# Four reorderings around the routing of a mixture of experts: weight splits, a gate's activation, two matmuls and two result adds

## The chip, the cores and the metric

The kernel runs on one core of one Trainium2 chip. The metric is the device time of one launch in microseconds (us), lower is better. The program is written engine by engine: TensorE (PE) multiplies, VectorE (DVE), ScalarE (ACT) and GpSimd (POOL) do the rest, SyncE (SP) issues transfers. Each engine runs its own instruction list in order and waits on semaphores that the others raise.

## The reference, cut to what matters

The reference is one layer: a cross attention, a state-space block beside an MLP, and then a mixture of experts on 1024 tokens of 512 features. Only the last part is touched. With `h` the normalised tokens:

```python
logits = h @ gate_weight.T                       # 8 experts
scores = softmax(logits)
topk_w, topk_i = group_limited_topk(scores)      # best 2 of 4 groups, then best 2 experts
g = einsum('th,nfh->ntf', h, gate_w); u = einsum('th,nfh->ntf', h, up_w)
e = einsum('ntf,nhf->nth', silu(g) * u, down_w)  # F = 352
routed = einsum('nth,tn->th', e, wmat)
shared = silu(h @ sh_gate_w.T) * (h @ sh_up_w.T) @ sh_down_w.T   # FS = 704
x = x + routed + shared
```

## The kernel before, in words

`phase_experts` handles the mixture as 39 steps of 128 tokens each. Steps 0 to 7 apply the first half of the shared expert's 704 features to the eight token tiles (weight set 0), steps 8 to 30 apply the routed experts to 23 tiles of tokens sorted by expert (sets 1 to 8), and steps 31 to 38 apply the other half of the shared expert (set 9). A step is `gate(j)`, `turn_hidden`, `up(j)`, `down(j)` on PE: twelve matmuls of 352 columns, twelve more, three transposes of the hidden rows, nine matmuls of 512 columns. Every product is made of three passes (high by high, high by low, low by high; lines 43 to 45), so every operand is split into a high and a low part. PE's list is software pipelined: at index `j` it runs `gate(j+1)`, `turn_hidden(j)`, `up(j+1)`, `down(j)`.

For each step ACT makes the activation of the gate (`gated`, line 2259) and the high part of the turned hidden rows (`hidden_hi`, line 2265); DVE makes the product of gate and up (`product`, line 2321), the low part of the hidden rows (`hidden_lo`, line 2325), and adds the step's result to `x` (`keep_results`, line 2354). `down(j)` waits for `hidden_lo(j)` (`hlo_ok`), and because the result has two buffers, for `keep_results(j-2)` (`y_ok`).

The routing is spread between the first steps. PE makes the logits during step 0. DVE's routing comes in pieces, `route.vector(v, m)`: m = 0 softmax, m = 1 groups, m = 2 the comparison of experts (lines 1910 to 1912), the choice (1917 to 1919) and running sums (1944), m = 3 the place of each token (1951 to 1965), m = 6 the tables of tiles, m = 5 the weights. Between m = 2 and m = 3 PE does two small matmuls, `tensor_places` (lines 1867 and 1870). At the end of m = 3 the slots are known (`slot_ok`), and POOL issues 16 indirect transfers of 256 KB each (line 2124) that write the normalised rows to their slots in memory. SP waits for all 16, then loads the first four sorted tiles (line 2081). PE turns the first of them (`turn_rows(0)`, line 2210) at index 6, between `up(7)` and `down(6)`; nothing behind it on PE can start before.

Weights arrive in one raw buffer of three pieces (gate, up, down). ACT makes the high part and DVE the low part of sets 0 and 1 (`split`, lines 2282 to 2285 and 2359 to 2363), POOL those of later sets, beginning after its scatters. SP issues the load of a piece of set k+1 when that of set k has been split (`piece_free`, lines 2070 to 2074). Set 1's three pieces are split by ACT at indices 1, 2 and 3 and by DVE at indices 2, 3 and 4, so the gate and up pieces of set 2 are loaded then.

Of the kernel before, what the change touches and what calls it, by code (L numbers as in the profile page):

```python
# [1802 lines left out]
NW, RING = 3, 3  # L1803
# [13 lines left out]
def route_programs(n, far, d, g):  # L1817
# [77 lines left out]
    def vector(v, m):  # L1895
# [39 lines left out]
                                 grank[:].rearrange("p t (g o) -> p t g o", o=1).to_broadcast([P, TT, NG, NE // NG]), ALU.mult))  # L1935
        if m == 2:
            compare(masked, NE)
            fewer_than_two(chosen, NE).then_inc(chosen_ok, 1)
            v.wait_ge(chosen_ok, 1)
            v.wait_ge(pads, 3)  # L1940
            for i in range(3):
                a, far_back = counted[i], 2 ** i
                out = counted[i + 1][:, 2 * far_back:2 * far_back + TT, :] if i < 2 else upto[:]
                v.tensor_tensor(out, a[:, far_back:far_back + TT, :], a[:, 0:TT, :], ALU.add).then_inc(summed, 1)
                v.wait_ge(summed, i + 1)
            link(v.tensor_tensor(masked[:], chosen[:], masked[:], ALU.mult))
        if m == 3:
            v.wait_ge(pos_ready, 1)
            places, held_by = psum[:, LB, 0:TT * NE].rearrange("p (t e) -> p t e", e=NE), psum[:, LB, TT * NE:(TT + 1) * NE]
            full = compared[:, 0, 0:NE * EXT].rearrange("p (e j) -> p e j", j=EXT)  # L1950
            link(v.tensor_tensor(full, held_by.rearrange("p (e o) -> p e o", o=1).to_broadcast([P, NE, EXT]), steps_of[:], ALU.is_gt))
            link(v.tensor_reduce(tiles[:], full, AX_X, ALU.add))
            over = compared[:, 0, 0:NE * NE].rearrange("p (e f) -> p e f", f=NE)
            link(v.tensor_tensor(over, before[:], tiles[:].rearrange("p (o f) -> p o f", o=1).to_broadcast([P, NE, NE]), ALU.mult))
            link(v.tensor_reduce(start[:], over, AX_X, ALU.add))

            link(v.scalar_tensor_tensor(out=pos[:], in0=start[:].rearrange("p (o e) -> p o e", o=1).to_broadcast([P, TT, NE]),
                                        scalar=float(SLOTS), in1=places, op0=ALU.mult, op1=ALU.add))

            link(v.scalar_tensor_tensor(out=held[:], in0=pos[:], scalar=-float(NT * SLOTS), in1=chosen[:], op0=ALU.add, op1=ALU.mult))  # L1960
            link(v.tensor_reduce(slot_f[:, 0, :], held[:], AX_X, ALU.min))
            link(v.tensor_scalar(slot_f[:, 0, :], slot_f[:, 0, :], float(NT * SLOTS), None, ALU.add))
            link(v.tensor_tensor(held[:], pos[:], chosen[:], ALU.mult))
            link(v.tensor_reduce(slot_f[:, 1, :], held[:], AX_X, ALU.max))
            v.tensor_copy(slot[:], slot_f[:]).then_inc(slot_ok, 1)
# [38 lines left out]
def phase_experts(nc, d, g, far, scan):  # L2004
# [8 lines left out]
    with ExitStack() as ctx:  # L2013
# [134 lines left out]
        @block.tensor  # L2148
        def _(pe):
            place = {}  # L2150

            def tokens(j):
                if routed(j):
                    return [a[:, (j - TT) % 2, :, :] for a in (tT_hi, tT_lo)]
                t = j % TT if j < TT else j - TT - NT
                return [a[:, :, t * P:(t + 1) * P] for a in (xT_hi, xT_lo)]

            def find_weights(j):
                if j == 0:
                    pe.wait_ge(first_ok, 2)  # L2160
                if j == TT:
                    pe.wait_ge(route.tables_ok, 1)
                if routed(j):
                    r = j - TT
                    need = pe.value_load(route.order[0:1, 0, r:r + 1], min_val=NW, max_val=NW * NE)
                    at = pe.value_load(route.order[0:1, 1, r:r + 1], min_val=0, max_val=RING - 1)
                    place[j] = bass.ds(at, 1)
                    pe.wait_ge(w_ok, need)
                else:
                    place[j] = slice(0, 1)  # L2170
                    if j == TT + NT:
                        pe.wait_ge(w_ok, NW * LAST)

            def features(j, i, bank):
                hi, lo = tokens(j)
                for dc in range(DC):
                    m = passes(pe, psum[:, bank + j % 2, 0:FE], hi[:, dc, :], lo[:, dc, :],
                               *(a[:, place[j], i, dc, :].rearrange("p o f -> p (o f)") for a in (w1_hi, w1_lo)),
                               dc == 0, dc == DC - 1)
                return m  # L2180

            def gate(j):
                find_weights(j)
                if routed(j):
                    pe.wait_ge(xlo_ok, j - TT + 1)

                wait(pe, s_ok, j - 1)
                features(j, 0, GB).then_inc(g_ready, 1)

            def up(j):  # L2190

                wait(pe, h_ok, j - 1)
                features(j, 1, UB).then_inc(u_ready, 1)

            def turn_hidden(j):
                pe.wait_ge(h_ok, j + 1)

                wait(pe, hlo_ok, j)
                f0 = 0
                for c, wd in enumerate(WD):  # L2200
                    m = pe.transpose(psum[0:wd, HB, c * P:(c + 1) * P], h[:, f0:f0 + wd], g["ident"][:])  # L2201
                    f0 += wd
                m.then_inc(ht_ready, 1)

            def turn_rows(r):
                pe.wait_ge(x_in[r % XR], 16 * (r // XR + 1))

                wait(pe, xlo_ok, r)
                for c in range(DC):
                    m = pe.transpose(psum[:, XB, c * P:(c + 1) * P], x_rows(r)[:, c * P:(c + 1) * P], g["ident"][:])  # L2210
                m.then_inc(xt_ready, 1)

            def down(j):
                if j == 0:
                    pe.wait_ge(first_ok, NW)
                pe.wait_ge(hlo_ok, j + 1)

                wait(pe, y_ok, j - 1)
                for c, wd in enumerate(WD):
                    m = passes(pe, psum[:, DB + j % 2, :], hT_hi[0:wd, c, :], hT_lo[0:wd, c, :],  # L2220
                               *(a[0:wd, place[j], c, :].rearrange("p o k -> p (o k)") for a in (w2_hi, w2_lo)),
                               c == 0, c == NC - 1)
                m.then_inc(dn_ready, 1)
            scan.tensor(pe)

            pe.wait_ge(scan.o_ok, TT - 1)
            norm.transpose_tile(pe, TT - 2)
            route.tensor_first(pe, 0)

            pe.wait_ge(scan.ms_ok, TT)  # L2230
            gate(0)
            norm.transpose_tile(pe, TT - 1)
            up(0)
            pe.wait_ge(norm.lo_done, TT)
            route.tensor_first(pe, 1)
            for j in range(STEPS):
                if j + 1 < STEPS:
                    gate(j + 1)
                if j == 0:

                    pe.wait_ge(scan.o_ok, TT)
                turn_hidden(j)
                if j == 0:
                    route.tensor_logits(pe)
                if j + 1 < STEPS:
                    up(j + 1)
                if j == 1:
                    route.tensor_places(pe)
                if routed(j + 2):
                    turn_rows(j + 2 - TT)  # L2250
                down(j)

        @block.scalar
        def _(act):
            def gated(j):
                act.wait_ge(g_ready, j + 1)

                wait(act, h_ok, j)
                act.activation(s[:], psum[:, GB + j % 2, 0:FE], ACT.Silu).then_inc(s_ok, 1)  # L2259
# [30 lines left out]
            norm.high_part(act, TT - 2)  # L2290
            act.wait_ge(scan.o_ready, TT)
            split(0, 2)
            gated(0)
            norm.high_part(act, TT - 1)
            route.scalar_first(act)
            for j in range(STEPS):
                if j + 1 < STEPS:
# [5 lines left out]
                    store_results(j - 1 - TT)  # L2303
                if j:
                    hidden_hi(j)
                if j - 1 in range(NW):
                    split(1, j - 1)
                if routed(j + 2):
                    r = j + 2 - TT
                    rows_hi(r)  # L2310
# [4 lines left out]
        def _(v):  # L2315
# [64 lines left out]
            split(0, 2)  # L2380
            norm.low_part(v, TT - 1)
            product(0)
            later = {0: 2, 1: 3, 2: 6, 3: 5}
            for j in range(STEPS):
                hidden_lo(j)
                if j == 0:
                    route.vector(v, 0)
                    route.vector(v, 1)
                if j + 1 < STEPS:
                    product(j + 1)  # L2390
                if j in later:
                    route.vector(v, later[j])
                if j - 2 in range(NW):
                    split(1, j - 2)
                if routed(j + 2):
                    rows_lo(j + 2 - TT)
                t = j - TT - NT
                if t >= 1:
                    v.wait_ge(y_ok, j)
                    add_back(t - 1)  # L2400
                    if t == TT - 1:
                        add_back(t)
                keep_results(j)


def second_columns(nc, ctx, tag):
# [160 lines left out]
```

## Time and profile before

| | |
|---|---|
| median of 3 runs | 1013.42 us (1009.63 to 1014.2) |
| profiled execution | 1011.37 us, span 1009.5 us |
| PE busy | 956.6 us, 95% |
| DVE, ACT, POOL busy | 530.1, 413.0, 453.4 us |
| experts begin, end | about 735 us to the end of the span |

The span is what the trace covers of the profiled execution; what lies around it is 1.87 us. A row of a timeline gives the start of an instruction, its duration, engine, line, operation, output and inputs, and in brackets the idle time of the engine before it with what ended it. Successive instructions of one engine can overlap by about 0.1 us, and PE's matmuls overlap by about half.

### The profile page before, as it was taken

The numbers are of one execution on the slowest core, as the hardware profiler recorded it, in microseconds if no ns is written. First come the engines' busy times: TensorE is split into PE (matmuls) and PEld (weight loads), VectorE is DVE, ScalarE is ACT, GpSimd is POOL, SyncE is SP. The second block draws the span as 40 slices with busy tenths as digits, with TensorE's granted clock in tenths as the row PEclk, the third lists the DMA queues.
The fourth block names the chain that finished last, engine by engine and source line by source line (L and its number), as shares of the span: only waits on it lengthen the run. The fifth ranks groups of instructions, "written<-read, shape, count | busy, mean of one in ns | idle before, by whom it ended". The sixth has DMA issues, their size and how long they took to land. (4 is left out here: it accounts for less than half of the span.)

```text
span 1009.5 us, 15936 instructions
## 1 busy us (share of the span) xinstructions
PE 956.6 (95%) x5497; PEld 807.7 (80%) x5497; DVE 530.1 (53%) x975; ACT 413.0 (41%) x956; POOL 453.4 (45%) x489
## 2 busy tenths in 40 slices
PE   6999977999899989999999999989999999999987
PEld 5777756888778868888888988767779899999977
DVE  4443358777788735454444223338866333333335
ACT  1444458777878724343222233543332122222111
POOL 1798866555667510000000303137607978990041
PEclk9999999999999999999999999999999999999989
DMA  7499813111111105223310025220016656751142
GB/s 248 159 269 266 239 55 95 43 43 38 38 32 41 46 1 188 84 83 101 125 45 21 14 59 156 88 100 2 23 65 210 224 194 204 231 184 50 52 145 96
DMA packets 79003, 109.92 MB, mean 109 GB/s; under 512 B 14224, under 2 KB 46992, under 8 KB 78928
## 3 DMA queue, kind: packets, MB, share of 16 engines
q1 hardware_dynamic: 66288, 82.18, 26.7%
q10 hardware_dynamic: 10080, 18.35, 5.2%
q0 software_dynamic: 2560, 8.39, 2.5%
q8 instruction: 46, 0.75, 0.3%
q14 instruction: 29, 0.24, 0.1%
HBM read 83.13 MB, written 25.77 MB: 108 GB/s over the span
## 5 line engine op out<-in xcount | busy, mean ns | idle before, releaser
L43 PE MATMUL psum<-second_xT_hi,second_w_hi 128*128 128x512 f32 x272 | 106.8, 393 | 4.9 <-PEq L74 2.9
L45 PE MATMUL psum<-second_xT_hi,second_w_lo 128*128 128x512 f32 x272 | 106.0, 390 | 0.0
L44 PE MATMUL psum<-second_xT_lo,second_w_hi 128*128 128x512 f32 x272 | 106.0, 390 | 0.0
L1239 POOL TENSOR_TENSOR all_x<-all_x,mlp_raw 128x512 f32<-128x512 f32 x8 | 10.0, 1288 | 173.1 <-DVE all_x L1741 173.1
L2259 ACT ACTIVATE moe_s<-psum 128x352 f32<-128x352 f32 x39 | 18.1, 465 | 156.1 <-PE psum L45 136.8
L2325 DVE TENSOR_TENSOR moe_hT_lo<-psum,moe_hT_hi 128x384 fp32r<-128x384 f32 x39 | 21.7, 558 | 83.0 <-ACT moe_hT_hi L2265 83.0
L43 PEld LDWEIGHTS psum<-second_xT_hi,second_w_hi 128*128 128x128 f32 x272 | 51.0, 188 | 17.4 <-issue 3.5
L1696 ACT ACTIVATE mlp_s<-psum,mlp_side 128x512 f32<-128x512 f32 x32 | 21.8, 682 | 100.2 <-PE psum L45 100.2
L43 PE MATMUL psum<-moe_w_hi,moe_tT_hi 128*128 x184 | 61.3, 333 | 0.0
L1741 DVE TENSOR_TENSOR all_x<-all_x,psum 128x512 f32<-128x512 f32 x64 | 43.8, 686 | 31.6 <-PE psum L45 31.2
L45 PEld LDWEIGHTS psum<-second_xT_hi,second_w_lo 128*128 128x128 f32 x272 | 51.1, 188 | 10.8
L44 PEld LDWEIGHTS psum<-second_xT_lo,second_w_hi 128*128 128x128 f32 x272 | 51.1, 188 | 10.5
L45 PE MATMUL psum<-moe_w_hi,moe_tT_lo 128*128 x184 | 59.2, 322 | 0.0
L44 PE MATMUL psum<-moe_w_lo,moe_tT_hi 128*128 x184 | 59.0, 320 | 0.0
L43 PE MATMUL psum<-moe_w_hi,moe_hT_hi 128*128 (+3 forms) x117 | 49.2, 421 | 5.7 <-DVE moe_hT_lo L2325 5.7
L43 PE MATMUL psum<-q_G_hi,att_cT_hi 128*128 128x512 f32 x128 | 52.9, 413 | 0.9 <-DVE all_x L1037 0.9
L2106 POOL TENSOR_TENSOR moe_w_lo<-far_raw,moe_w_hi 128x1408 fp32r<-128x1408 f32 x16 | 51.9, 3244 | 0.0
L44 PE MATMUL psum<-q_G_lo,att_cT_hi 128*128 128x512 f32 x128 | 50.5, 395 | 0.0
L45 PE MATMUL psum<-mix_wo_hi,mix_wo_lo 128*128 128x512 f32 x128 | 49.9, 390 | 0.0
L43 PE MATMUL psum<-mix_wo_hi 128*128 128x512 f32 x128 | 49.9, 390 | 0.0
L44 PE MATMUL psum<-mix_wo_lo,mix_wo_hi 128*128 128x512 f32 x128 | 49.8, 389 | 0.0
L1735 DVE TENSOR_TENSOR mix_wo_lo<-mlp_s,mix_wo_hi 128x512 fp32r<-128x512 f32 x32 | 22.1, 691 | 51.5 <-ACT mix_wo_hi L1702 51.5
(344 smaller groups left out, 2868.3 us busy)
## 6 DMA issues: line engine op xcount, KB each, us to landing
kv_all<-all_x ACTq DMA_DIRECT2D x28, 256.0 KB, 4.9
far_raw<-in_eg SPq DMA_DIRECT2D x10, 704.0 KB
far_raw<-in_eu SPq DMA_DIRECT2D x10, 704.0 KB
slot_rows<-mix_W SPq DMA_DIRECT2D x23, 256.0 KB, 5.9
slot_out<-far_rows ACTq DMA_DIRECT2D x23, 256.0 KB, 2.3
far_raw<-in_ed SPq DMA_DIRECT2D x10, 512.0 KB
far_rows<-slot_rows ACTq DMA_DIRECT2D x19, 256.0 KB, 3.3
second_raw<-in_w_feat SPq DMA_DIRECT2D x18, 256.0 KB, 3.5
```

The source lines that it names most:

```text
L43: e.matmul(out, hi_l, hi_r, start=first, stop=False)
L44: e.matmul(out, hi_l, lo_r, start=False, stop=False)
L45: return e.matmul(out, lo_l, hi_r, start=False, stop=last)
L1239: pool.tensor_tensor(g["x"][:, t, :], g["x"][:, t, :], b2, ALU.add).then_inc(x_plus, 1)
L1696: act.activation(s1[:, m % 2, :], psum[:, UP + m % 4, :], ACT.Gelu_apprx_tanh, bias=side[:, p, c:c + 1]).then_inc(act_ok, 1)
L1735: v.tensor_tensor(h_lo[:, c, half * HALF:(half + 1) * HALF], s1[:, m % 2, :], h_hi[:, c, half * HALF:(half + 1) * HALF].bitcast(F32), ALU. ...
L1741: v.tensor_tensor(x[:, t, :], x[:, t, :], psum[:, DN + t % 4, :], ALU.add).then_inc(dn_ok, 1)
L2106: pool.tensor_tensor(w1_lo[:, u, i, :, :], raw1[:, i, :, :], w1_hi[:, u, i, :, :].bitcast(F32), ALU.subtract).then_inc(w_ok, 1)
L2259: act.activation(s[:], psum[:, GB + j % 2, 0:FE], ACT.Silu).then_inc(s_ok, 1)
L2325: v.tensor_tensor(hT_lo[:], psum[:, HB, 0:NC * P].rearrange("p (c k) -> p c k", k=P), hT_hi[:].bitcast(F32), ALU.subtract).then_inc(hlo_ok, 1)
```

## The change

Four lists are reordered; nothing is computed that was not computed before.

```diff
@@ route_programs.vector
         if m == 2:
             compare(masked, NE)
+        if m == 3:
             fewer_than_two(chosen, NE).then_inc(chosen_ok, 1)
...
-        if m == 3:
+        if m == 4:
             v.wait_ge(pos_ready, 1)
@@ tensor
-                if j == 1:
-                    route.tensor_places(pe)
                 if routed(j + 2):
                     turn_rows(j + 2 - TT)
                 down(j)
+                if j == 1:
+                    route.tensor_places(pe)
@@ scalar
             split(0, 2)
+            split(1, 0)
             gated(0)
             norm.high_part(act, TT - 1)
+            split(1, 1)
             route.scalar_first(act)
...
-                if j - 1 in range(NW):
-                    split(1, j - 1)
+                if j == NW:
+                    split(1, NW - 1)
@@ vector
             product(0)
-            later = {0: 2, 1: 3, 2: 6, 3: 5}
+            split(1, 0)
+            split(1, 1)
+            later = {0: 2, 1: 4, 2: 6, 3: 5}
             for j in range(STEPS):
                 hidden_lo(j)
                 if j == 0:
                     route.vector(v, 0)
                     route.vector(v, 1)
+                if j == 1:
+                    route.vector(v, 3)
                 if j + 1 < STEPS:
                     product(j + 1)
                 if j in later:
                     route.vector(v, later[j])
-                if j - 2 in range(NW):
-                    split(1, j - 2)
+                if j == NW + 1:
+                    split(1, NW - 1)
+                if j == 1:
+                    keep_results(0)
...
-                keep_results(j)
+                if j:
+                    keep_results(j)
```

So on DVE the order after the comparison becomes: `hidden_lo(1)`, choice and sums (now m = 3), `product(2)`, places (now m = 4), `keep_results(0)`, `keep_results(1)`. On PE `down(1)` stands ahead of the two matmuls of `tensor_places`. The gate and up pieces of set 1 are split before index 0 on both engines; its down piece stays at index 3 on ACT and 4 on DVE.

## Rows read from the trace of the kernel before

**Rows 1.** Chain that ended last, 735 to 800 us: start, duration, what.

```profile
782.36 3.92 DMA slot_rows<-far_rows,moe_slot
786.29 2.78 DMA far_rows<-slot_rows
```

**Rows 2.** Timeline of PE around the places, and the first turned rows.

```profile
749.20 0.32 PE L43 MATMUL psum<-moe_w_hi,moe_xT_hi 128*128 128x352 f32 x1
...
753.23 0.32 PE L45 MATMUL psum<-moe_w_hi,moe_xT_lo 128*128 128x352 f32 x1
...
755.00 0.43 PE L1870 MATMUL psum<-moe_upto,far_earlier 128*128 128x64 f32 x2 [0.34 <-DVE moe_upto L1944]
756.45 0.50 PE L43 MATMUL psum<-moe_w_hi,moe_hT_hi 128*128 128x512 f32 x1 [1.01 <-DVE moe_hT_lo L2325]
...
758.64 0.32 PE L43 MATMUL psum<-moe_w_hi,moe_xT_hi 128*128 128x352 f32 x1
...
789.12 0.66 PE L2210 MATMUL psum<-all_ident,far_rows 128*128 128x128 f32 x4 [0.98 <-DMA far_rows<-slot_rows]
```

**Rows 3.** Timeline of DVE through the routing.

```profile
745.17 0.56 DVE L2325 TENSOR_TENSOR moe_hT_lo<-psum,moe_hT_hi 128x384 fp32r<-128x384 f32 x1 [4.98 <-ACT moe_hT_hi L2265]
...
752.52 0.69 DVE L1917 TENSOR_TENSOR moe_compared<-moe_compared 128x512 f32<-128x512 f32 x1
...
755.24 0.69 DVE L2354 TENSOR_TENSOR all_x<-all_x,psum 128x512 f32<-128x512 f32 x1
755.84 0.55 DVE L2325 TENSOR_TENSOR moe_hT_lo<-psum,moe_hT_hi 128x384 fp32r<-128x384 f32 x1
756.31 0.51 DVE L2321 TENSOR_TENSOR moe_h<-moe_s,psum 128x352 f32<-128x352 f32 x1
756.74 0.22 DVE L1951 TENSOR_TENSOR moe_compared<-psum,far_steps_of 128x64 f32<-128x64 f32 x1
...
759.24 0.17 DVE L1965 CAST moe_slot<-moe_slot_f 128x16 uint32<-128x16 f32 x1
```

**Rows 4.** Timeline of ACT: the first gate, and the hidden rows of step 1.

```profile
737.23 0.47 ACT L2259 ACTIVATE moe_s<-psum 128x352 f32<-128x352 f32 x1 [2.64 <-PE psum L45]
...
752.17 0.49 ACT L2265 ACTIVATE moe_hT_hi<-psum 128x384 fp32r<-128x384 f32 x1
```

**Rows 5.** Timeline of POOL: four of the 16 scatters, the first and the longest.

```profile
759.72 1.22 POOL L2124 DMA_INDIRECT slot_rows<-far_rows,moe_slot  x1 [23.81 <-DVE moe_slot L1965]
...
766.49 2.35 POOL L2124 DMA_INDIRECT slot_rows<-far_rows,moe_slot  x1 [0.30 <-issue]
...
771.68 2.11 POOL L2124 DMA_INDIRECT slot_rows<-far_rows,moe_slot  x1 [0.30 <-issue]
...
776.65 1.58 POOL L2124 DMA_INDIRECT slot_rows<-far_rows,moe_slot  x1 [0.30 <-issue]
```

**Rows 6.** Timeline of DVE: low parts of set 1, beside the scatters.

```profile
766.38 1.62 DVE L2359 TENSOR_TENSOR moe_w_lo<-far_raw,moe_w_hi 128x1408 fp32r<-128x1408 f32 x1
...
771.33 1.62 DVE L2359 TENSOR_TENSOR moe_w_lo<-far_raw,moe_w_hi 128x1408 fp32r<-128x1408 f32 x1
...
776.17 1.22 DVE L2361 TENSOR_TENSOR moe_w_lo<-far_raw,moe_w_hi 128x1024 fp32r<-128x1024 f32 x1
777.31 0.68 DVE L2362 TENSOR_TENSOR moe_w_lo<-far_raw,moe_w_hi 96x512 fp32r<-96x512 f32 x1
```

**Rows 7.** View of the tile `slot_rows`: durations in ns (minimum, median, maximum), and landings.

```profile
L2124 POOL DMA_INDIRECT slot_rows<-far_rows,moe_slot x16: 965/971/2345, 759.7 to 782.4; - x16
...
DMA to landing us min/median/max: 2.6/5.4/7.0
```

**Rows 8.** DMA busy tenths from 728 to 748 us, a digit per 0.5 us.

```profile
DMA  0005569961008399810000589991000000000000
```

**Rows 9.** Timelines of ACT and PE near 970 us.

```profile
969.05 0.46 ACT L2259 ACTIVATE moe_s<-psum 128x352 f32<-128x352 f32 x1 [8.53 <-remote]
...
971.61 0.80 PE L43 MATMUL psum<-moe_w_hi,moe_hT_hi 128*128 128x512 f32 x1 [3.47 <-DVE moe_hT_lo L2325]
...
975.62 0.49 PE L43 MATMUL psum<-moe_w_hi,moe_xT_hi 128*128 128x352 f32 x1
```

**Rows 10.** Window: us, busy us of PE, PEld, DVE, ACT, POOL; granted clock; DMA share; GB/s.

```profile
971.00:972.00 1.00, 0.39 (x1) 0.39 (x2) 1.00 (x3) 0.00 (x0) 0.00 (x0) 0.50 0.05 21
```

## The prediction

> **What bounds the kernel now.** I began with the chain that ended last, which says where the end is set. Through the experts it lies on PE, except between about 744 and 789 us: there it runs through the routing on DVE, the 16 scatters on POOL, the landing of the last scatter (3.92 us) and the load of the first sorted tile (2.78 us) [rows 1]. Then I read PE's timeline for what this costs PE. It stands idle in two places. The first is around the places. The last matmul of `up(2)` starts at 753.23 and frees the array 0.16 later, at 753.39; `down(1)` begins only at 756.45 and `gate(3)` at 758.64 [rows 2]. `tensor_places` waits for DVE's choice and sums, and `down(1)`, queued behind it, then waits for `hidden_lo(1)`. The second is `turn_rows(0)`: 0.98 us until 789.12, for the sorted rows [rows 2]. So two paths arrive at 789 almost together, PE 1 us ahead of the scatters. Speeding one alone is worth 0 (PE) or at most 1.0 us (scatters); the change touches both.
>
> **PE: `down(1)` ahead of the places.** It needs `hidden_lo(1)`. ACT ends the high part at 752.17 + 0.49 = 752.66 [rows 4]. In the new order DVE has done only the comparison by then, which ended where L1917 begins, 752.52 [rows 3]. So `hidden_lo(1)` runs from about 752.69 to 753.24 and PE sees it 0.06 later (before, 756.39 and 756.45): 753.30, ahead of 753.39. `down(1)` starts without a wait and takes 758.64 - 756.45 = 2.19 [rows 2], or 2.1 without its slow first matmul: until 755.5.
>
> DVE goes on 0.47 after it started `hidden_lo(1)` (755.84 to 756.31 [rows 3]), at 753.16. Choice, sums and the masked weights take 755.24 - 752.52 = 2.72, so `product(2)` starts at 755.88, and the last sum, one instruction of 0.26 before that, is in at 755.60. The second matmul of the places starts at about 755.7, bound by PE's own queue as much as by DVE, and takes 0.43 [rows 2]. `gate(3)` starts at about 756.1, where it was 758.64: 2.5 us earlier.
>
> **What is late next.** `gate(3)`, `turn_hidden(2)` and `up(3)` take what their forerunners took, 753.39 - 749.20 = 4.19 [rows 2], so `down(2)` could begin at 760.3. It waits for `hidden_lo(2)`, which on DVE now stands behind the places and two result adds. `product(2)` 755.88, places from 755.88 + 0.43 = 756.31 (PE's answer is in at 756.15), `keep_results(0)` after 759.24 - 756.74 + 0.08 = 2.58, at 758.89, `keep_results(1)` 0.60 later, `hidden_lo(2)` at 760.09, done at 760.64 [rows 3]. PE starts `down(2)` at 760.70, plus 0.1 for a first matmul after a wait. Before it started at 758.64 + 4.19 = 762.83. The gain on PE is 2.1 us, not 2.5. `keep_results(0)` itself is needed by `down(2)`, at 759.6: in time. From index 2 on DVE has two splits of 1.62 fewer, so no later `hidden_lo` is late. PE comes to `turn_rows(0)` at 789.12 - 0.98 - 2.1 = 786.05.
>
> **The splits ahead of the routing.** ACT stands idle 2.64 us before its first gate at 737.23 [rows 4]. The load of set 1's gate piece was issued when DVE had split that of set 0, and its transfer is the first burst, over by 733.0; the second, the up piece, is over by 737.0 [rows 8]. A gate piece takes ACT 1.4 us: from 734.6 to 736.0, before 737.23. The up piece, after the last norm tile at 738.3, ends before 740, and ACT's next work comes at 742.4. DVE stands idle 4.98 us before 745.17, from 740.2 [rows 3], and the two low parts take 2 x 1.62 = 3.24 [rows 6]: done by 743.5, with 1.7 us in hand. Both cost nothing here. Without that cover each 1.62 would fall on the routing chain. The issue of set 2's gate and up pieces on SP moves with them, from 768 and 773 to about 742 and 743.5; from 742 to 748 the DMA engines were idle [rows 8], and nothing in SP's list stands between.
>
> **The scatters.** A scatter takes 0.97 us at the median [rows 7] and 0.30 to the next. Three are long: 2.35, 2.11 and 1.58 [rows 5], 1.38 + 1.14 + 0.61 = 3.13 us over the rest. Each began while DVE was making a low part of set 1, and each ended 0.84 us after that instruction: 766.38 + 1.62 = 768.00 and 768.84; 772.95 and 773.79; 777.39 and 778.23 [rows 5, 6]. Three times the same 0.84 is no chance. The change takes the first two splits away, so 2.52 go. The third stays at index 4, 2.1 us earlier, at 774.05 to 775.27. On the new grid a scatter begins at 774.9 to 775.0 and would be held 0.15 to 0.3 instead of 0.61. I count nothing for it, and bound it between 0.5 gained and 0.5 lost.
>
> The Trainium skill ("SBUF — State Buffer", the section on the two physically separate sides) says that a VectorE instruction with two SBUF inputs and a GpSimd one share a port pair by an exclusive lock, held for the whole instruction. By its words whoever starts first wins and the other fully blocks; here the second instruction of the third split (777.31) did not hold POOL again, since the scatter was under way, and its own 0.68 was not stretched. If a scatter fell between the two parts and were held by the second one, the third split would cost up to 0.9 us instead of 0.3. That bound would put the first row at 786.9 at the latest.
>
> The slots are known 0.43 us earlier (L1951 at 756.31, not 756.74 [rows 3]). The last scatter is issued at 782.36 - 0.43 - 2.52 = 779.4. Its landing took 3.92 then, while the loads of set 2 shared the engines; the least of the 16 was 2.6 [rows 1, 7]. Now only the down piece's load falls in the train. Between 2.6 and 3.92 I take 3.1, nearer to the least, since two of three loads are gone: 782.5. The first sorted tile is in 2.78 later, at 785.3, within 784.5 and 786.6 over both bounds and the third split. PE comes at 786.05. So PE is likely not held, or for a few tenths, and both idle spots go.
>
> **Sum.** PE resumes at 786.05 instead of 789.12: 3.1 us, 2.5 at worst by these bounds. Behind it everything that PE could wait for is POOL's splitting, which starts 2.9 us earlier as well, and no wait for weights was seen. So 1009.5 becomes 1006.4 in span and 1011.37 becomes 1008.3 in the profiled execution's own time. That execution lies 2.05 us below the median of the runs, so for the median 1013.42 - 3.1 = 1010.3.
>
> **Rivals.**
> *The wait only moves.* PE gains 2.1, but the rows come as late as before but for 0.43, because the long scatters have another cause (a descriptor buffer that fills, say) and would recur. Against it stand the three equal 0.84. It gives 0.4 us: 1013.0.
>
> *The hole at 970 goes.* ACT's gate activation came at 969.05 after 8.53 us of waiting for something the trace calls remote, PE waited 3.47 [rows 9], and afterwards its granted clock stood at 0.50, that is 1.2 GHz [rows 10]: the nine matmuls of `down` took 975.62 - 971.61 = 4.01 us [rows 9] instead of 2.19, and the next gate began slow too (0.49 instead of 0.32 a matmul), some 2.5 us. In all 6 us. It lies beside POOL's gathers and is not touched, but it is no data wait that I can name, and may come and go by execution: 3.1 + 6 gives 1004.3. The Trainium skill ("Runtime: NRT & Kernel Launch", instruction fetch mechanics) says engines fetch instructions by a DMA queue of their own and mostly hide it; this hole is what an unhidden fetch would look like, and no row proves it.
>
> *Slower: such a hole opens in another place.* The loads of set 2 now run at 742 to 747, a stretch in which no data moved and in which the chain runs through ACT and DVE. If one engine's remote wait of the kind of [rows 9] falls there, or the one near 970 grows to twice its size, 6 us are lost against 3.1 won: 1016.3. It decides from a hold of 3.1 us on the chain. Against it: between 728 and 742 loads ran beside the same engines [rows 8] without one.
>
> **How the numbers follow.** The forecast (2.5 to 3.4 us gained) has 0.62, the moved wait and values between 0.3 and 2.5 us 0.20, the vanished hole 0.10, the new hole 0.08. The likeliest case is 1010.3. The runs of before spread over 4.6 us, more than the gain, so the median of a few can lie 2 us to either side. The range that leaves out 2 in 10 is 1005.5 to 1013.5. Half a per cent is 5.1 us, about what tells from no change. The forecast lies inside it; with the spread of the runs 0.12 of it goes beyond, and with the vanished hole faster gets 0.22. Slower gets 0.06 of the new hole and the spread, and 0.72 is left for no change.
>
> **What would show it.** Right: on PE, `down(1)` about 0.1 us behind the last matmul of `up(2)`, `gate(3)` near 756.1, an idle spot of about 0.4 us ahead of `down(2)` released by L2325, and none or under 0.5 us ahead of L2210 at about 786. On POOL, a first scatter at 759.3, no scatter of 2.1 to 2.4 us, at most one over 1.3, and a train of 20 instead of 22.6 us to the start of the last. On SP, the loads of set 2 at about 742 and 743.5. Wrong: long scatters without a split beside them; a wait of over 1 us ahead of L2210; ACT's first gate after 737.3 or `hidden_lo(0)` after 745.3, which would mean that the early splits are on the path.

## The result, and the profile after

The changed kernel takes 1022.18 us (median of 8 runs, 1019.21 to 1024.27), the kernel before 1013.81 us beside it (8 runs, 1009.63 to 1027.34). The ratio is 1.0084, 95% interval 1.0064 to 1.0105: slower by 8.4 us, where 3.1 us less was forecast. The profiled execution took 1023.44 us with a span of 1021.6 us; its mean granted clock was 0.984, where that of before was 0.994.

I compared the start of the same PE instruction in both traces, after minus before:

| point | before | after | difference |
|---|---|---|---|
| first 370 us | | | -0.9 to +0.9 |
| 700 to 755 us | | | +4.5 |
| `gate(3)` | 758.64 | 760.49 | +1.85 |
| `down(2)` | 762.83 | 765.32 | +2.49 |
| `down(4)` | 775.48 | 788.25 | +12.8 |
| `turn_rows(0)` | 789.12 | 802.32 | +13.2 |
| end | 1009.5 | 1021.6 | +12.1 |

First the 4.5 us that lie far ahead of the change. The difference is 0.9 us at 370 us; another 1.5 and 2.8 us come in two stretches in which the granted clock of the changed kernel stood at 0.50 (1.2 GHz), which the windows of both kernels show (0.7 is made good between them). Each line is a stretch, its length, the busy time (and count) of PE, weight load, DVE, ACT and POOL, then clock, DMA share and GB/s. The first block is after, the second before, over the same work:

```profile
378.43:381.84 3.41, 3.11 (x7) 2.48 (x8) 1.40 (x5) 0.00 (x0) 1.94 (x3) 0.50 0.47 125
675.39:682.21 6.82, 6.11 (x15) 4.94 (x16) 4.97 (x5) 2.46 (x3) 6.09 (x6) 0.50 0.83 307
```

```profile
377.00:381.00 4.00, 3.26 (x17) 2.73 (x17) 1.40 (x5) 0.00 (x0) 2.09 (x3) 1.00 0.45 126
672.00:679.00 7.00, 5.97 (x85) 4.74 (x86) 5.29 (x4) 4.08 (x4) 4.74 (x5) 1.00 0.95 331
```

The instructions there are the same in both kernels, and such slow stretches come in some executions of before too (e10 below, which is the kernel before, was at 0.50 from 671.1 to 677.9); I leave them out of the account of the change. Within the change's own part, 4.5 us (4.55 just ahead of `gate(3)`) has to be taken off every time of after.

There the forecast's steps came as written. PE's timeline after (start, duration, engine, line, operation, output and inputs, in brackets the idle time before and its end):

```profile
760.28 0.40 PE L1870 MATMUL psum<-moe_upto,far_earlier 128*128 128x64 f32 x2
760.49 0.41 PE L43 MATMUL psum<-moe_w_hi,moe_xT_hi 128*128 128x352 f32 x1
...
765.32 0.50 PE L43 MATMUL psum<-moe_w_hi,moe_hT_hi 128*128 128x512 f32 x1 [0.43 <-DVE moe_hT_lo L2328]
...
771.50 0.32 PE L45 MATMUL psum<-moe_w_hi,moe_xT_lo 128*128 128x352 f32 x1
...
773.52 0.39 PE L45 MATMUL psum<-moe_w_hi,moe_hT_lo 96*128 96x512 f32 x1
...
775.51 0.33 PE L45 MATMUL psum<-moe_w_hi,moe_xT_lo 128*128 128x352 f32 x1
775.67 0.49 PE L2202 MATMUL psum<-all_ident,moe_h 128*128 128x128 f32 x3
...
777.78 0.32 PE L45 MATMUL psum<-moe_w_hi,moe_xT_lo 128*128 128x352 f32 x1
788.25 0.80 PE L43 MATMUL psum<-moe_w_hi,moe_hT_hi 128*128 128x512 f32 x1 [10.16 <-DVE moe_hT_lo L2328]
```

Both waits around the places [rows 2] are gone: `gate(3)` gained 4.55 - 1.85 = 2.7 us, `down(2)` waits 0.43 us, and 4.55 - 2.49 = 2.1 us of gain stay. The last line is the loss: PE stands idle for 10.16 us ahead of `down(4)`, where before it had no wait. `up(5)` ended at 778.1, and PE's next instruction had to wait.

POOL's groups by line give the count, least, median and longest duration in ns, and the first and last start; and SP's queue the issues of set 2's loads:

```profile
L2125 POOL DMA_INDIRECT slot_rows<-far_rows,moe_slot x16: 968/972/1225, 763.9 to 783.3; - x16
```

```profile
746.29 0.34 SPq L2071 DMA_DIRECT2D far_raw<-in_eg  x1
747.82 0.33 SPq L2071 DMA_DIRECT2D far_raw<-in_eu  x1
```

The long scatters of [rows 5] are gone. The 16 now form one train without a break, a start each 1.28 us, 19.4 us to the start of the last instead of 22.64.

What held PE? DVE's `hidden_lo(4)` was released by ACT, which waited for PE's transposes and `gate(5)`. Timelines of ACT and DVE through the hole:

```profile
786.76 0.46 ACT L2260 ACTIVATE moe_s<-psum 128x352 f32<-128x352 f32 x1 [14.84 <-remote]
```

```profile
774.02 0.52 DVE L2324 TENSOR_TENSOR moe_h<-moe_s,psum 128x352 f32<-128x352 f32 x1 [2.96 <-remote]
...
778.31 0.69 DVE L2357 TENSOR_TENSOR all_x<-all_x,psum 128x512 f32<-128x512 f32 x1 [2.35 <-remote]
```

Compare them with when PE ended that work, in the fence of PE above. `up(4)` ended at 771.8 and DVE's product of it came at 774.02; `down(3)` ended at 773.9 and its result add came at 778.31; `gate(5)` ended at 775.8 and ACT's activation came at 786.76, 11 us later and 2.5 us after the last scatter's instruction (783.32 + 0.97). So the data was there and the word of it was late. "Remote" is how the trace writes a release that it can't put down to an instruction: [rows 9] shows the same, 8.53 us, near 970. That hole too lies in such a train, 10 gathers (indirect transfers that read the sorted results back) at 1.25 us, without a break but not quite without a stall: the sixth took 1.35 us instead of 0.95. After the change it is still there, the sixth gather first, then ACT:

```profile
975.66 1.38 POOL L2146 DMA_INDIRECT far_rows<-slot_out,moe_slot  x1 [0.30 <-issue]
977.34 0.95 POOL L2146 DMA_INDIRECT far_rows<-slot_out,moe_slot  x1 [0.30 <-issue]
```

```profile
982.16 0.47 ACT L2260 ACTIVATE moe_s<-psum 128x352 f32<-128x352 f32 x1 [8.61 <-remote]
```

The windows show that apart from POOL no engine was busy for more than 1.05 of 10 us in the new hole, and what followed. Of PE only the end of one matmul lies in the first; over the second the clock was at 0.50, and a 128x512 matmul took 0.63 us where 0.39 is usual:

```profile
778.00:788.00 10.00, 0.09 (x1) 0.00 (x0) 1.05 (x2) 0.84 (x2) 4.85 (x5) 0.66 0.42 159
```

```profile
781.20:791.44 10.24, 3.19 (x8) 2.52 (x9) 2.72 (x4) 0.84 (x2) 3.50 (x4) 0.50 0.26 97
```

The hole cost 10.3 us (2.49 to 12.8), the slow matmuls behind it 1.5; the wait for the first sorted rows (0.98 in [rows 2]) was gone, which gave 1.0 back. The sum over the change's part: -2.1 + 10.3 + 1.5 - 1.0 = +8.7 us; a shorter slow stretch behind the late hole takes it to 7.6 at the end (12.1 - 4.5). The medians differ by 8.4.

### The profile page after: what moved, and what is told of

It reads as the page before. It is cut to its first block and busy times, and to the rows that moved or that the text cites. A ratio compares the mean times of both kernels' runs of the same rounds, so it can differ in the third digit from the quotient of the medians.

```text
span 1021.6 us, 15937 instructions
## 1 busy us (share of the span) xinstructions
PE 961.2 (94%) x5497; PEld 811.1 (79%) x5497; DVE 531.6 (52%) x975; ACT 413.3 (40%) x956; POOL 451.0 (44%) x489
```

## The experiments

Four chips are on record for the experiments: Q (e1 to e4), R (e5 to e8, e17, e18), S (e9 to e12) and T (e13 to e16). Which one the pair above ran on is not; it is called P, and may be a fifth or one of these. "Before" is always the kernel before on the same chip. The theory after the first pair: POOL's unbroken train of indirect transfers holds back PE's signals (the semaphore counts by which ACT and DVE learn that a matmul is done); before, three scatters stalled behind DVE's splits [rows 5, 6] and so broke it. Rivals: the order of the lists does it, or set 2's loads at 742 us.

**Halves of the change.** e1 keeps the new order with the splits where they were; e2 does only the early splits:

```diff
@@ e1, against the changed kernel (ACT; DVE alike)
-            split(1, 0)
-            split(1, 1)
-                if j == NW:
-                    split(1, NW - 1)
+                if j - 1 in range(NW):
+                    split(1, j - 1)
```

> Only the reordering of DVE's and PE's lists around the places; set 1 is split where it was before, so its three low parts still interrupt the scatters. Theory T1 (PE's signals are held when POOL issues more than about six scatters without a break): the scatters keep their breaks of 1.38, 1.14 and 0.61 us, no hole near 778, PE 2.1 us earlier up to the wait for the sorted rows, of which 0.4 remains: 1013 against 1013.8 of before, ratio 0.9995. Theory T2 (the new order itself opens the hole, whatever the scatters do): a hole of about 10 us ahead of down(4), 1022. Theory T3 (early loads of set 2 open it): as T1.

> Only the two early splits; the order around the places is that of before. T1: the scatters come in one train of 1.28 us each, a hole of some 10 us on PE with 1.2 GHz behind it opens as in the changed kernel, 12 us less 1 us of the rows' wait: 1022 to 1025. T2: no hole, scatters 2.5 us shorter, 1 us gained: 1012.8. T3: as T1.

e1: 1009.55 against 1010.64 us, ratio 0.9991 [0.996, 1.0022]. e2: 1020.64, ratio 1.0125 [1.006, 1.0191]. The splits alone bring the whole loss. In e1 three scatters stalled again, and PE has no wait between `down(2)` and the rows; in e2 PE waited 8.54 us. POOL of e1 (two of its three long ones), then ACT of e2:

```profile
764.95 1.50 POOL L2125 DMA_INDIRECT slot_rows<-far_rows,moe_slot  x1 [0.30 <-issue]
...
770.59 1.49 POOL L2125 DMA_INDIRECT slot_rows<-far_rows,moe_slot  x1 [0.30 <-issue]
```

```profile
780.37 0.46 ACT L2259 ACTIVATE moe_s<-psum 128x352 f32<-128x352 f32 x1 [13.21 <-remote]
```

This leaves two differences, the loads that move with the splits and the unbroken train.

**Breaks in the trains.** e3 is the changed kernel, in which POOL does two of its own splits of set 2 (1.37 us each) after the 5th and 10th scatter instead of after the 16th. e4 is the kernel before with a copy of 1.37 us, whose result nobody reads, after the 3rd, 6th and 9th gather of each late train.

```diff
@@ e3, after a scatter on POOL
+                    if TOP * t + i + 1 in (5, 10):
+                        split(2, -1 - (5, 10).index(TOP * t + i + 1))
@@ e4, after a gather on POOL
+                    if TOP * t + i + 1 in (3, 6, 9):
+                        pool.tensor_copy(w1_hi[:, 1 + i, (t & 1), :, :], raw1[:, 0, :, :])
```

> The changed kernel, with POOL's high parts of set 2's gate and up pieces (1.37 us each) moved between its scatters, after the fifth and after the tenth. Loads of set 2 stay early. T1: no hole near 778; the last scatter is issued 2.7 us later than in the changed kernel, PE waits about 2 us for the rows: gain of 0.5 to 1.5 us over before, 1012.5. T2 and T3: the hole stays, 1022 or more.

> The kernel before, with a copy of 128x1408 elements on POOL (1.37 us, its result is never read) after gathers 3, 6 and 9 at the end. T1: the hole of 3.5 us near 970 and the 1.2 GHz behind it go: about 6 us, 1008. If the hole there comes from something else than an unbroken run of indirect transfers: it stays, 1013.8, or 1015 if the gathers' delay shows.

e3: 1010.49 us, ratio 0.9992 [0.9957, 1.0027], on the chip on which e2 lost 10 us; no hole near 778, with set 2's loads as early as in e2 (issued at 740.03 and 741.57; e2 739.57 and 741.10). So the early loads alone don't open the hole. DVE's third split made one more stall there, a scatter of 1.40 us. The price of the breaks is a wait of 1.09 us for the rows. e4: 1008.22 us, ratio 0.9972 [0.9943, 1.0001]; the hole near 970 is gone, and across that stretch its PE gained 6.3 us on the profile of before (5.3 us behind it at 965, 0.9 ahead at 980; another chip). The medians differ by 2.4 us only, and the interval reaches 1.0001, so the forecast gain of 6 us is not shown for the whole kernel. POOL of e4 in the gathers, and PE of e1, which on the same chip kept the hole:

```profile
964.20 0.95 POOL L2145 DMA_INDIRECT far_rows<-slot_out,moe_slot  x1 [0.30 <-issue]
965.14 1.38 POOL L2148 CAST moe_w_hi<-far_raw 128x1408 fp32r<-128x1408 f32 x1
966.70 0.97 POOL L2145 DMA_INDIRECT far_rows<-slot_out,moe_slot  x1 [0.17 <-issue]
```

```profile
970.15 0.80 PE L43 MATMUL psum<-moe_w_hi,moe_hT_hi 128*128 128x512 f32 x1 [3.54 <-DVE moe_hT_lo L2326]
```

**How much of a break.** Four versions of the changed kernel: e5 one break of 1.37 us after scatter 8; e6 a POOL instruction of 0.20 us after scatters 5 and 10; e7 no break, but each scatter waits until the third before it has landed; e8 the breaks of e3 and e4 together.

```diff
@@ e6
+                    if TOP * t + i + 1 in (5, 10):
+                        pool.tensor_tensor(rest[:, t:t + 1], norm.power[:, 0:1], norm.power[:, 0:1], ALU.add)
@@ e7
+                    m = TOP * t + i
+                    wait(pool, scattered[m % 3], 16 * (m // 3))
```

> The changed kernel with one break of 1.37 us (POOL's high part of set 2's gate piece) after the eighth scatter, so two runs of eight. In the changed kernel PE's signals were first late at the seventh or eighth scatter, and at the seventh of the gathers. If the length of an unbroken run decides (T1): PE is held only for the last one or two of each eight, under 2 us in all, no 10 us hole. If the hold comes from the whole amount of scatters in a stretch whatever the breaks: the hole stays near 10 us.

> The changed kernel with one tiny POOL instruction (one element a partition, 0.2 us) after scatters five and ten. If any other POOL instruction between scatters ends the run (something is drained when the kind of work changes): no hole. If a break must last (the pace decides): the hole of about 10 us stays.

> The changed kernel with three semaphores for the scatters; scatter m waits until scatter m-3 has landed (2.6 to 3 us after its issue, so at 1.28 us a scatter the wait costs little). If the hold comes from too many scatters in flight: no hole. If it comes from the pace of issue alone (T1 proper): the pace stays 1.28 us and the hole stays, about 1022.

> The changed kernel with the two breaks among the scatters (useful work) and three among the gathers. T1: what the two single kernels gave adds up, 2.9 us and 5.5 us in the experts' stage: ratio to before 0.992, 1002.5 at a before of 1010.6. If the gathers' breaks only paid because the rest was as before: 0.997.

| | median, us | before | ratio | holes |
|---|---|---|---|---|
| e5 | 1004.20 | 1007.60 | 0.9963 [0.9938, 0.9987] | none |
| e6 | 1004.88 | 1007.60 | 0.9968 [0.994, 0.9997] | none |
| e7 | 1006.07 | 1007.60 | 0.999 [0.9965, 1.0014] | none |
| e8 | 1005.69 | 1007.60 | 0.9976 [0.9956, 0.9996] | none |

All looked like cures, which was too good: no kernel had even the hole near 970, though the gathers of e5 to e7 have no break, and before itself was 3 to 6 us faster than on P and Q. So chip R may not make such holes at all, and the four prove nothing without the changed kernel beside them.

**The same on chip S, with controls.** e9 is the changed kernel, e10 the kernel before, e11 is e7's kernel, e12 is e6's.

> The changed kernel itself, on another chip than its first profile. In the last four runs, all on one chip, the late hole near 970 was gone too, though nothing near it was changed: the holes may belong to some chips alone. If the hole is the kernel's (T1): ratio to before 1.008, PE held some 10 us near 778. If it is the chip's: on a chip without it, the changed kernel runs 2 to 3 us under before, ratio 0.997.

> The kernel before itself, profiled on the same chip as e9. It tells whether this chip shows the late hole near 970 (ACT's gate activation 3 us late beside the gathers). Time: ratio 1.0 to before. With a hole here and none near 970 in e5 to e8, the chips differ; without one here, this chip is of their kind.

> The kernel of e7 (scatter m waits for the landing of m-3) on the same chip as e9. If e9 shows the hole and this doesn't, the number in flight or the wait itself opens it, not the pace. If both show it, the pace does, and e7's good result was its chip's. If neither shows it, this chip says nothing on it.

> The kernel of e6 (a 0.2 us POOL instruction after scatters five and ten) on the same chip as e9. Where e9 shows the hole: none here if any other POOL instruction ends the run of scatters, the same 10 us hole if a break has to last.

e9: 1023.15 us, ratio 1.0081 [1.0032, 1.013]: the first result again. e11: 1022.8, ratio 1.0117 [1.0045, 1.0189], and e12: 1021.31, ratio 1.0102 [1.0016, 1.0188], of two runs each. PE of e9, then of e11, then of e12:

```profile
785.89 0.79 PE L43 MATMUL psum<-moe_w_hi,moe_hT_hi 128*128 128x512 f32 x1 [9.73 <-DVE moe_hT_lo L2328]
```

```profile
785.02 0.79 PE L43 MATMUL psum<-moe_w_hi,moe_hT_hi 128*128 128x512 f32 x1 [9.74 <-DVE moe_hT_lo L2331]
```

```profile
785.71 0.79 PE L43 MATMUL psum<-moe_w_hi,moe_hT_hi 128*128 128x512 f32 x1 [9.75 <-DVE moe_hT_lo L2331]
```

Three holes of one size: neither the limit of three in flight nor two instructions of 0.20 us change it. The limit was a weak test, though: POOL waited for a landing once in e11, 0.47 us ahead of the thirteenth scatter, so the train was nearly the same, and it shows that the hole needs no more than about three scatters in flight. The two "cures" of chip R were the chip.

e10 was meant as a plain control: 1011.5 us, ratio 0.9978 [0.9929, 1.0027]. But its profiled execution (span 1017.6, clock 0.984) had the hole, in the kernel before, here in pieces: PE was 1.7 us behind the first profile at 770.6, 8.9 at `down(4)` and 11.9 at `down(5)`. Its POOL has no scatter over 1.23 us, and PE's signals were late; POOL, then ACT of e10:

```profile
766.61 0.97 POOL L2124 DMA_INDIRECT slot_rows<-far_rows,moe_slot  x1 [0.30 <-issue]
767.88 0.96 POOL L2124 DMA_INDIRECT slot_rows<-far_rows,moe_slot  x1 [0.30 <-issue]
769.15 1.23 POOL L2124 DMA_INDIRECT slot_rows<-far_rows,moe_slot  x1 [0.30 <-issue]
```

```profile
771.38 0.46 ACT L2259 ACTIVATE moe_s<-psum 128x352 f32<-128x352 f32 x1 [6.82 <-remote]
782.93 0.46 ACT L2259 ACTIVATE moe_s<-psum 128x352 f32<-128x352 f32 x1 [9.25 <-remote]
```

PE and DVE of e10 say why the stall failed to come:

```profile
756.70 0.79 PE L43 MATMUL psum<-moe_w_hi,moe_hT_hi 128*128 128x512 f32 x1 [1.01 <-DVE moe_hT_lo L2325]
```

```profile
767.88 1.66 DVE L2359 TENSOR_TENSOR moe_w_lo<-far_raw,moe_w_hi 128x1408 fp32r<-128x1408 f32 x1
```

PE's `down(1)` ran slow (0.79 where 0.50 is usual [rows 2]), so DVE's first split began at 767.88 instead of 766.38 [rows 6]. It ended at 769.54 and found a scatter issued 0.39 before that, which it held for 0.26 us, not for the 1.38 of [rows 5]; the second split began at 779.89, when the last scatter had been issued. A stall that depends on where a DVE instruction falls on a grid of 1.28 us is a matter of luck, and without it the kernel before has the hole as well. It also settles the two rivals better than e3 does: this hole opened in the old order, with set 2's loads late (769.57 and 781.55).

It was no single case. Of the executions of before, 2 of 8 on P, 1 of 25 on Q and 6 of 22 on S took over 1017 us; of 85 on R and T none took over 1011.5. Only e10's was profiled, so that the others had the hole too is a guess.

**Chip T, with the changed kernel as control.** e13 is the changed kernel, e14 is e3's, e15 e5's and e16 e8's.

> The changed kernel as control of its chip: with the hole of about 10 us the three kernels beside it can be judged, at a ratio near 1.008; without it (a chip of the kind of e5 to e8) the ratio is 0.997.

> The kernel of e3 (breaks of 1.37 us after scatters 5 and 10). If breaks of such a length keep PE's signals free (T1): no hole where e13 has one, ratio 0.997 to 1.000. If e3's good result was its chip's: the hole as in e13, 1.008.

> The kernel of e5 (one break of 1.37 us after scatter 8). T1 with a limit of about six or seven: signals late by 1 to 3 us around scatters 7, 8, 15 and 16, between e13 and e14, ratio 1.000 to 1.004. If only breaks as such count: as e14. If breaks do nothing: as e13.

> The kernel of e8 (breaks among scatters and gathers). T1: neither hole, ratio 0.992 where e13 has both. If breaks do nothing: as e13, or 1 us more.

| | median, us | before | ratio |
|---|---|---|---|
| e13 changed | 1004.09 | 1007.57 | 0.9962 [0.9935, 0.9988] |
| e14 | 1006.11 | 1007.57 | 0.9986 [0.9965, 1.0006] |
| e15 | 1005.86 | 1007.57 | 0.9986 [0.9965, 1.0008] |
| e16 | 1004.3 | 1007.57 | 0.9974 [0.9952, 0.9996] |

Here the changed kernel is faster than before, by 3.5 us, with the very same train. POOL's group with the landings of the 16 scatters, then PE at `down(2)` and at the first sorted rows, then ACT near 979, all of e13:

```profile
L2125 POOL DMA_INDIRECT slot_rows<-far_rows,moe_slot x16: 968/972/1224, 757.0 to 776.6; - x16
...
DMA to landing us min/median/max: 2.7/2.8/4.8
```

```profile
758.41 0.50 PE L43 MATMUL psum<-moe_w_hi,moe_hT_hi 128*128 128x512 f32 x1 [0.40 <-DVE moe_hT_lo L2328]
...
783.53 0.60 PE L2211 MATMUL psum<-all_ident,far_rows 128*128 128x128 f32 x4
```

```profile
979.04 0.47 ACT L2260 ACTIVATE moe_s<-psum 128x352 f32<-128x352 f32 x1 [5.44 <-PE psum L45]
```

No hole, no wait for the rows, and near 979 ACT is released by PE after its usual 5.4 us. Against the profile of before, PE is 2.35 us ahead just before the change's part and 5.59 at `turn_rows(0)`: 3.2 us gained there. The breaks, which are good for nothing here, cost e14 a wait of 1.5 us for the rows and e15 one of 0.2.

**A last pair.** e17 is the changed kernel and e18 e3's kernel, to have both on a chip with holes.

> The changed kernel as control once more: e13 to e16 fell on a chip without the hold (the changed kernel had no hole and ran at 0.996 of before). On a chip with it: hole of about 10 us, ratio 1.008. Without: 0.996.

> The kernel of e3 beside the control e17. If e17 shows the hole: none here if 1.37 us breaks after five and ten scatters prevent it (T1), ratio 0.997 to 1.000; the same hole if e3's good result was its chip's. If e17 shows none: 0.998, and this pair says nothing on the hole.

They fell on chip R: e17 1004.87 us against 1007.32, ratio 0.9968 [0.994, 0.9996], no hole; e18 1005.48, ratio 0.9993 [0.9969, 1.0018]. So the changed kernel has no hole on R either, and e5 to e8 were no cures; it does not give the pair that I wanted.

**What the traces lost.** A further look at the traces shows a second difference between the chips. Each of the 16 scatters raises the semaphore `scattered` (e7 and e11 have three) by 16 in steps of 1, and where none is lost each step has a record in the trace, 256 in all.

| profiles | records of 256 |
|---|---|
| ten on R and T | 255 or 256 |
| four on P and Q with breaks or stalls (before, e1, e3, e4) | 160, 98, 111, 161 |
| six on P, Q and S with the hole (after, e2, e9, e10, e11, e12) | 55 to 67 |

That is why the landing line of e13 has no counterpart in the profile after. On P, Q and S records get lost during the trains, most where the hole is. So the theory has a rival that no run tests: the crowded path may be that of the trace's own records. Every execution timed here carries a span and a granted clock, which a trace gives; whether a launch without recording has the hole is not known.

## Why the prediction was wrong

*What held.* On PE `gate(3)` stands 0.2 us behind the second matmul of the places, the wait ahead of `down(2)` is 0.43 us (0.4 forecast), and the gain there 2.1 us (2.1). The scatters: no scatter over 1.23 us (at most one over 1.3), 19.4 us of train (20); but the third split, which was to fall beside them, came only at 788, behind the hole. The loads of set 2 at 746.29 and 747.82, less 4.5 us 741.8 and 743.3 (742 and 743.5). The wait of 0.98 us for the rows gone. The splits on ACT and DVE delayed nothing: `hidden_lo(0)` began at 749.71, that is 745.2 (745.17 [rows 3]). On chips T and R the sum came out as well: 3.2 us in e13's profile and ratios of 0.9962 and 0.9968, that is 3.8 and 3.2 us of 1007.57 and 1007.32, where 3.1 was forecast.

*Slips that changed nothing.* The prediction took 2.6 us for "the least of the 16" landings. The line in [rows 7] covers every transfer of the tile `slot_rows`; none of the 16 scatters has a landing in that trace. In e13 they took 2.7 to 4.8 us and the last was seen by SP after 3.9 (776.63 to 780.51), where the sum has 3.1. With 3.9 the rows come at 786.1, as PE does, so that slip costs under 0.1 us. And "2.5 at worst" leaves out the sum's own later bound of 786.9, by which it is 2.2.

*The Trainium skill's rule* ("SBUF — State Buffer", the section on the two physically separate sides) stood beside the three long scatters. Here the trace agrees: without a low part of set 1 on DVE beside them none was long, and in e1, with these back, the long ones were (1.50, 1.49, 1.73 us). That such a stall is nothing but cost was my own reading; the page doesn't say it.

*What failed.* The step "The scatters" counted the 2.52 us of stalls as gain and asked nothing of what a train without them does to the others. The stalls were also the only breaks in it. The row that said so was in my hands: the remote wait near 970 [rows 9] stands inside ten gathers at 1.25 us without a break (one stall of 0.40), and the prediction says "it lies beside POOL's gathers and is not touched", takes it for a thing that comes and goes, and even puts up a rival in which it goes. What the runs show in its place: with the stalls gone, PE stood idle for 10.16 us ahead of `down(4)`. The rival that came true is "such a hole opens in another place". It has the kind right (a remote wait of the kind of [rows 9], 1.2 GHz behind it), but not the place or the cause: it ties it to set 2's loads at 742 to 747, and it came at 778 in the scatters, as long as the train went on. Priced 6 us, it cost 10.3 + 1.5 us; given 0.08, it stands in both profiles of the changed kernel on chips P and S.

*How sure the cause is.* Shown: the early splits bring the loss (e1, e2 on one chip). Their loads are not it: e3 has them early without a hole, e10 late with one. The new order isn't needed (e2, e10). More than about three scatters in flight aren't needed (e11), and pauses of 0.20 us don't help (e12). A gather train with breaks of 1.37 us loses its hole (e4, e1). On a chip with holes an unbroken train had one in all six profiles (the first pair's, e2, e9, e10, e11, e12), and a train with breaks or stalls of 0.5 us and more had none in four (before on P, e1, e3, e4). That is a pattern over ten profiles; that the missing breaks are the cause is argued from it. Not shown: that breaks alone cure the changed kernel, since no chip with holes ran e3's or e5's kernel beside the changed one, and e3 and e2 differ in the order too. Nor what the scatters and PE's signals share, whether recording has a part in it, nor why chips P, Q and S make such holes and R and T don't: the lost records are those by which the path could be read. Which chip a run would get was unknown ahead, so a forecast from the profile of before alone, a chip with a hole near 970, had to reckon with it.

*Another reading that doesn't hold.* The prediction cited the Trainium skill ("Runtime: NRT & Kernel Launch", instruction fetch mechanics) for the hole near 970 as an unhidden fetch. From 960 to 972 us the trace of before has no instruction packet at all. In the new hole there is one, of 1.1 us at 776.95; e9 has it too, 0.94 us at 775.0. But e17, the same kernel on a chip without holes, has it at the same point of PE's work, 0.94 us at 776.0. The packets' lines for 3 us around it, after and then e17:

```profile
q8 instruction: 1, 0.02, 2.3%
```

```profile
q8 instruction: 1, 0.02, 1.9%
```

The transfer of the fetch takes as long in e17, without a hole, as in e9, with one, so this fetch doesn't explain a wait from 775.8 to 786.8.

*A better version?* On chips without holes the changed kernel itself is the best that ran (0.9962, 0.9968); on T the breaks cost it 0.2 to 2.0 us in the medians; on R e5 was 0.7 us lower and e18 0.6 higher, within the spread. On a chip with holes the best was e4 (0.9972), whose interval reaches 1.0001. The changed kernel with both breaks (e8, e16) never ran on such a chip, so I can't name one that beats both everywhere.

## What to carry to other kernels

A stall that you remove may have been what kept a queue from running unbroken: before counting it as gain, look for another place of the trace in which the same instructions already run without a break, and read what the other engines wait for there. Suspect that a wait called remote that ends with another engine's train of DMA issues belongs to that train. When a cure works, run the disease beside it on the same chip: e6 looked like 0.3% gained (e7 like 0.1%), and both were 1% lost on another. And count the records of a trace before reading a wait in it: where records are missing, the recording may have a part in the wait.

## What the runs showed of the hardware

- On chips P, Q and S, 16 indirect scatters issued by POOL every 1.28 us without a break went with late completions of TensorE as seen by ACT and DVE, later as the train ran: after the change 2.2 us at 774, 4.4 at 778.3, 11 at 786.8. On R and T the same train delayed nothing, and the whole kernel before was faster there by 3 to 6.5 us (1007.3 to 1007.6 against 1010.6 to 1013.8).
- Of the 256 steps by which the scatters raise their semaphore, traces on R and T hold 255 or 256, traces on P, Q and S 55 to 67 with the hole and 98 to 161 without.
- Stalls of 0.5 us inside a scatter (e1) went with no hole; a stall of 0.26 us (e10) and instructions of 0.20 us between two scatters (e12) did not keep it away, nor did a limit of three in flight (e11), which bound once. One stalled gather (1.35 for 0.95 us at 962.62 before, 1.38 at 975.66 after) did not keep the later hole away either.
- A POOL indirect DMA with a VectorE instruction of two inputs beside it ended 0.84 us after that instruction [rows 5, 6]; e1 repeats it: 764.00 + 1.62 = 765.62, and the scatter ended at 766.45. So does e10: 769.54 and 770.38.
- With PE idle from 778.1, the granted clock stood at 0.50 from 781.2 and until 791.44, 3.2 us after work resumed at 788.25; behind a hole of the same length e12's matmuls were slow until 791.5, 5.8 us after 785.71.
